# Two attention layers, one core: another place for the copied tiles and another order of the small products

## The reference

```python
# layer 0
theta, phi = W_theta x + b_theta, W_phi x + b_phi            # 64 channels
f = softmax(theta^T phi / sqrt(64))                          # 1024 x 1024 per image
x = x + W_fuse (x f^T) + b_fuse
# layer 1
h = group_norm(x, 32 groups) * gn_w + gn_b
q, k, v = q_w h + q_b, k_w h + k_b, v_w h + v_b              # 128 channels
a = softmax(q^T k / sqrt(128))
x = x + p_w (v a^T) + p_b
```

## Time and profile before

| | |
|---|---|
| median of 3 runs | 1895.29 us (1894.0 to 1898.93) |
| profiled execution | 1903.5 us, span 1901.7 us |
| busy | PE 92%, PEld 63%, DVE 75%, ACT 76%, POOL 67% |
| SP's DMA queue | 286.08 MB, 74.4% of 16 engines |
| granted TensorE clock | 0.990 of full speed |

### The profile page before, as it was taken

How to read it: one execution, slowest core, us unless ns; L and a number is a source line. 1 busy time by engine, 2 the same in 40 slices (tenths; PEclk the granted TensorE clock), 3 DMA queues, 4 the chain that set the end, 5 groups by cost and what they waited for, 6 DMA issues and landing times.

```text
span 1901.7 us, 34446 instructions
## 1 busy us (share of the span) xinstructions
PE 1759.0 (92%) x8966; PEld 1191.6 (63%) x8966; DVE 1432.4 (75%) x1650; ACT 1441.4 (76%) x2152; POOL 1273.3 (67%) x1321
## 2 busy tenths in 40 slices
PE   4799999999999999999999999999999999999986
PEld 2466666666666666666666666666666666666654
DVE  4577778778777787777787777877777878777854
ACT  3577877777877777877877877877887877877854
POOL 2566776666776666776666776666776666776652
PEclk9899999999999999999999999999999999999998
DMA  3578777877878778778777778778777777778764
GB/s 77 101 144 151 158 151 165 160 150 157 163 145 172 157 151 160 158 150 169 151 156 158 156 155 170 146 160 159 149 162 164 153 156 157 148 157 168 140 126 95
DMA packets 860085, 286.33 MB, mean 151 GB/s; under 512 B 822304, under 2 KB 823200, under 8 KB 860064
## 3 DMA queue, kind: packets, MB, share of 16 engines
q1 hardware_dynamic: 860064, 286.08, 74.4%
HBM read 50.86 MB, written 17.04 MB: 36 GB/s over the span
## 4 chain that ended last, share of the span: by engine, by line
issue 24%; DVE 17%; DMA 16%; ACT 14%; PE 11%; POOL 9%; SPq 9%; DVEq 1%; ACTq 0%; POOLq 0%
DMA et<-pair 11%; SPq L340 7%; DVE neg_max L704 6%; PE o_ps L416 5%; DMA rden_dram<-rden 4%; ACT s_ps L610 3%; ACT pair L635 3%; DVE pair L721 3%; DVE phi L795 2%; PE s_ps L416 2%; PE s_ps L454 2%; DVE x L758 2%; ACT et L620 2%; DVE x_max L781 2%; PE m_ps L416 1%
## 5 line engine op out<-in xcount | busy, mean ns | idle before, releaser
L416 PE MATMUL o_ps<-et,v_hi 128*128 128x512 f16 x2048 | 699.0, 383 | 50.3 <-DVE x L758 31.2
L704 DVE TENSOR_REDUCE neg_max<-s_ps 128x1 f32<-128x1024 f32 x512 | 624.4, 1220 | 66.0 <-PE s_ps L416 56.0
L416 PEld LDWEIGHTS o_ps<-et,v_hi 128*128 128x128 f16 x2048 | 203.0, 99 | 303.4 <-issue 119.8
L416 PE MATMUL o_ps<-et,v_lo 128*128 128x512 f16 x1024 | 390.6, 381 | 0.0
L721 DVE SCALAR_TENSOR_TENSOR pair<-s_ps,pair 128x1024 f16<-128x1024 f32 x256 | 312.1, 1219 | 75.6 <-ACT pair L635 74.4
L416 PE MATMUL s_ps<-phi,theta 128*128 128x512 f32 x1024 | 331.1, 446 | 6.0 <-ACT e_copied L610 3.7
L610 ACT ACTIVATE s_ps<-s_ps,neg_max 128x1024 f32<-128x1024 f32 x256 | 277.3, 1083 | 58.5 <-DVE neg_max L704 57.8
L846 POOL TENSOR_TENSOR pair<-e_copied,pair 128x1024 f16<-128x1024 f32 x128 | 274.6, 2145 | 23.3 <-ACT pair L633 23.3
L715 DVE SCALAR_TENSOR_TENSOR et<-s_ps,et 128x1024 f16<-128x1024 f32 x128 | 156.7, 1224 | 170.5 <-ACT et L620 170.5
L935 POOL TENSOR_TENSOR x<-x,xr 128x512 f32<-128x512 f32 x64 | 81.5, 1274 | 288.0 <-DVE x L758 288.0
L635 ACT ACTIVATE pair<-s_ps 128x1024 f16<-128x1024 f32 x256 | 262.2, 1024 | 8.1
(11 more groups left out here) (113 smaller groups left out, 3076.9 us busy)
## 6 DMA issues: line engine op xcount, KB each, us to landing
rden_row<-rden_dram SPq DMA_DIRECT2D x128, 256.0 KB, 3.9
xs<-in_x SPq DMA_DIRECT2D x32, 512.0 KB, 4.0
phi<-phi SPq DMA_DIRECT2D x64, 256.0 KB, 3.2
out_y<-y_sb SPq DMA_DIRECT2D x64, 256.0 KB, 2.5
et<-pair SPq DMA_TRANSPOSE x384, 4.6
rden_dram<-rden SPq DMA_DIRECT2D x128, 2.0 KB, 1.5
w_f<-in_w_fuse_t SPq DMA_DIRECT2D x1, 64.0 KB, 3.1
ident_sb<-in_ident SPq DMA_DIRECT2D x1, 64.0 KB, 2.3
```

Of the source, the lines that this page charges most:

```text
L416: mm = pe.matmul(out, lhs_t, rhs, start=start and n == 0, stop=stop and n == len(terms) - 1)
L704: nc.vector.tensor_reduce(neg_max[:, t % 4:t % 4 + 1], s_ps[:, part(t), :], AX.X, ALU.max, negate=True).then_inc(s_max, 1)
```

## The change

PAIRS becomes 4. Copied tiles use place 0 and place 3 in turn (a new function `place`), and every wait for a transpose and every transpose goes by the place. In UNITS w0 and q1 change slots (7 and 8), mx moves from slot 14 to slot 11 and v0 from 15 to 14; STAGE follows. On POOL the halves of h_lo are made in slots 2 and 3 instead of 3 and 4; in slot 2 this stands ahead of the copied tile's rest. The scores of slot 12 wait for one split more, since q1 comes a slot later.

```diff
-PAIRS = 3
+PAIRS = 4
-UNITS = {0: "gn1", 1: "gn2", 2: "v1", 4: "k0", 5: "k1", 6: "q0", 7: "q1", 8: "w0", 9: "w1", 10: "tp0", 12: "tp1",
-         14: "mx", 15: "v0"}
-STAGE = {"v1": 0, "k0": 1, "k1": 0, "q0": 1, "q1": 0, "w0": 1, "w1": 0, "v0": 1}
+UNITS = {0: "gn1", 1: "gn2", 2: "v1", 4: "k0", 5: "k1", 6: "q0", 7: "w0", 8: "q1", 9: "w1", 10: "tp0", 11: "mx",
+         12: "tp1", 14: "v0"}
+STAGE = {"v1": 0, "k0": 1, "k1": 0, "q0": 1, "w0": 0, "q1": 1, "w1": 0, "v0": 1}
-H_LO_SLOTS = (3, 4)
+H_LO_SLOTS = (2, 3)
...
+    def place(s):
+
+        return PAIRS - 1 if s % GROUP == COPIED and s // GROUP % 2 else s % GROUP
+
     def same_pair(s):
 
-        return lambda g: int(tile_at(g) and g % GROUP == s % GROUP)
+        return lambda g: int(tile_at(g) and g % GROUP != TURNED and place(g) == place(s))
...
                     if s == PHASE + GROUP:
-                        pe.wait_ge(s_split, before(staged_at, it, 8))
+                        pe.wait_ge(s_split, before(staged_at, it, 9))
...
-                n, r = before(tile_at, it, t), t % GROUP
+                n, r = before(tile_at, it, t), place(t)
                 act.wait_ge(s_exp, n + 1)
 
                 act.wait_ge(s_pair_t[r], 16 * before(same_pair(t), it, t))
...
-                    pool.wait_ge(s_h32, before(h_at, it, s))
-                    pool.wait_ge(s_hhi, before(h_at, it, s))
+                    pool.wait_ge(s_h32, before(h_at, it, H_SLOT) + 1)
+                    pool.wait_ge(s_hhi, before(h_at, it, H_SLOT) + 1)
...
-                        rest(pair[:, COPIED, 1, :], e_copied[:, :], pair[:, COPIED, 0, :], s_copied)
+                        rest(pair[:, place(t), 1, :], e_copied[:, :], pair[:, place(t), 0, :], s_copied)
```

More of the change, by code:

```diff
@@ L340, in move @@
                 sp.dma_start_transpose(et[:, t // GROUP % 4, r, :, :],
-                                       pair[:, r, :, :].rearrange("q a n -> q (a n)")).then_inc(s_pair_t[r], 16)
+                                       pair[:, place(t), :, :].rearrange("q a n -> q (a n)")).then_inc(
+                                           s_pair_t[place(t)], 16)
             def reciprocals_out(it, s):
@@ L463, in values @@
                 if quarter == 0:
-                    for r in range(PAIRS):
-                        pe.wait_ge(s_pair_t[r], 16 * before(same_pair(r), it, first + GROUP))
+                    for t in range(first, first + TURNED):
+                        pe.wait_ge(s_pair_t[place(t)], 16 * before(same_pair(t), it, first + GROUP))
                     pe.wait_ge(s_tlo, before(turned_at, it, first + GROUP))
```

## The result

| | before | after |
|---|---|---|
| median of 4 runs each | 1895.32 us | 1910.43 us (1908.19 to 1911.94) |
| ratio after/before | | 1.0074, interval 1.0058 to 1.0091 |
| profiled execution | 1903.5, span 1901.7 | 1908.19, span 1906.4 |

The changed kernel is slower by 15 us, 0.7%. So I compare one steady stretch of each instead, from VectorE's maximum of tile 0 in image 3 to the same in image 30: 27 images. One row for before, then one for after; the columns are the stretch, its length, the busy time of PE, PEld, DVE, ACT and POOL, the granted clock, the DMA share and GB/s.

What follows compares the result with a forecast made beforehand. Bound: VectorE in slots 10 to 15, the SP queue's reciprocals and transposes from slot 2 to 6. Terms +1.13 − 0.61 + 0.35 − 0.04 − 0.05 = +0.78 per image, times 30 = +23 us: 1918, range 1882 to 1930.

Steps and rivals of the forecast that it cites:

- Slot 6: Slot 6's value products: the third transpose's landing practically bounds them, so removing ScalarE's wait gives only −0.04 us per image.
- the transposes are not the bound of slot 6: Rival in slot 6: TensorE regains waits before q0 and k0; +0.08 us per image, 1898 us, no change; chance 0.12.
- The handshake: Slots 11 and 12: mx waits for VectorE's phi, VectorE's bound for mx; tile 11's turned rest +1.13 us per image.
- long way over TensorE: From mx in slot 11 through value products, tp1 and ScalarE to tile 11's turned rest: 519.45 where 518.32 stood, +1.13.
- the gain before it: VectorE's 0.46 us idle before tile 9's rest goes, so phi ends at 513.01 instead of 513.47.
- Slot 15: VectorE's bound (0.21) and clamp with reciprocal (0.40) leave slot 15: −0.61 us per image.
- v0's move: v0 in slot 14 fills TensorE's 1.05 us of waiting, but TensorE waits again before tile 15's transposes: 0.
- The queue: SP queue: transposes and xs load come 0.40 later against the next image's reciprocals: +0.35 us per image, ends 0 and +0.50.
- The fixed-cost rival: SP queue: about 2 us fixed per DMA, queue term 0; +0.43 per image, 1908 us; chance 0.64 together with the forecast.
- w0, q1 and h's low half: w0 before q1 in slots 7 and 8: −0.05 us per image; h's low half first on POOL: 0.
- The handshake costs nothing: Rival in slot 11: VectorE has taken phi before TensorE reaches mx; −0.60 us per image, 1877 us; chance 0.13.
- The queue gets worse: Rival: the handshake costs 0.90 and the late transposes 0.50; +1.30 us per image, 1934 us; chance 0.07.

Runs made afterwards that it cites:

- e3_mx_only: The kernel before with only mx moved to slot 11 and v0 to slot 14: 1949.87 us, ratio to before 1.0260.
- e9_small_parts: The kernel before with only w0 and q1 exchanged and h's low half in slots 2 and 3: 1900.42 us, ratio to before 1.0007.
- e7_xs_late: The changed kernel with the next image's xs load issued in slot 4 of the SP queue instead of slot 1: 1897.06 us, ratio to before 0.9974.
- e4_phi_first: The changed kernel with VectorE taking tp0's theta and phi before tile 9's rest in slot 11: 1897.49 us, ratio to before 0.9980.

## Why the prediction was right, and where its sizes were off

The direction and the mechanism held; 1918 was 8 too slow. Step by step, per image:

- **Slot 6: the transposes are the bound, though 131 us of ScalarE's waiting goes.** Held. Landing to first value product was 0.23 in the mean before and is 0.09 in 26 of 27 images after. The step was sized −0.04 and measured −0.14 (−0.12 in the mean over all 27). I had taken 0.2 as the price of waiting for a landing. In fact it was the end of a second chain that was just behind the landing. The ScalarE of before in that image:

```profile
548.07 1.06 ACT L633 ACTIVATE pair<-e_copied 128x1024 f16<-128x1024 f32 x1 [1.41 <-DMA et<-pair]
549.03 0.67 ACT L583 ACTIVATE stage<-m_ps,vec 128x512 f32<-128x512 f32 x1
```

The second transpose lands just before 548.07, the stage copy ends at 549.70, q0's product starts at 549.75, and behind its three matmuls the value product at 550.56. After, q0's product starts at 552.20 and TensorE stands 0.76 before the value product. This is the slack that the removed wait left unused; the rival "the transposes are not the bound of slot 6" falls by it.

- **The handshake.** Forecast +1.13 from slot 10's normalisation to the turned rest, measured +0.97. Its long way over TensorE was forecast at 1.59 (1.13 + 0.46) and measured at 1.56, and VectorE's wait for the bound at 0.55 and measured 0.58 in every image. The step that was mis-sized is the gain before it: phi comes 0.60 earlier by the normalisation, not 0.46. VectorE's idle time before tile 9's rest was 0.50 in the mean over images (0.41 to 1.02); I had sized it from one image. The remaining 0.10 I did not trace. A slip in the working is small: it takes 0.98 from tp1's start to ScalarE's theta, where its rows give 1.02 (514.84 to 515.86).

- **Slot 15.** Forecast −0.61, measured −0.67. v0's move gave nothing else, as forecast: TensorE waits 1.23 before tile 15's transposes in every image (0.33 in the mean before), and they start no earlier after it. That is a reading of the timelines; no run moves v0 alone.

- **The queue.** Forecast +0.35, measured +0.31 at the third landing. That the two are so close is partly luck: the price was taken from two images of one kernel, and e3_mx_only, whose lead shrinks by 0.47 instead of 0.44, has 0.65. The fixed-cost rival fell, although its 1908 is nearer to the measured 1910 than my 1918: other terms moved the number there, and its own term, 0, is not what the queue shows. The time of the 2 KB out went from 2.29 to 2.58 with the load nearer, and to 1.72 where the load is elsewhere. The Trainium skill ("DMA: Bandwidth & Descriptors", section on queues, rings and completion order) says that a DMA engine's semaphore write lands only after its earlier writes; these numbers agree with it, and so do the landings of the 2 KB 0.35, 0.26 and 0.19 behind that of the load. The Trainium skill gives the rival's 2 us (same page, section on the anatomy of one DMA) for DMAs that GpSimd issues. Those here are issued by SP, and in slot 10, where everything ahead of them had landed, the 2 KB took 1.64 before and 1.63 after.

- **w0, q1 and h's low half.** Forecast −0.05 together, and e9_small_parts measures none. Tile 0's rest ends 2.0 later (10.85 to 12.82), where I had 1.8. h's low half costs only when the reciprocals come back early, as e7_xs_late shows.

The terms make +0.11 up to slot 10, +0.97 and −0.67: +0.41, where the forecast had +0.26, +1.13 and −0.61. Two thirds of the missing 0.37 lie in gains of the fourth place that I undersized (0.10 in slot 6, 0.14 before phi). "The handshake costs nothing" fell by the row of mx. "The queue gets worse" was right in kind for e3, where its term was 0.65.

One thing in the comparison of profiles is the clock's. Behind the maximum of image 31 the span goes on for 120.6 us before and 113.7 after, although little is changed there. e9_small_parts, whose steady part is that of before, takes 115.4. The rows of these ends (stretch, length, busy times, granted clock, DMA share, GB/s), for before and e9:

```profile
1781.10:1901.70 120.60, 97.41 (x452) 61.93 (x451) 63.35 (x69) 65.87 (x100) 62.87 (x67) 0.92 0.58 118
```

```profile
1781.20:1896.60 115.40, 91.54 (x451) 57.99 (x451) 63.22 (x68) 65.56 (x99) 62.79 (x67) 0.98 0.61 124
```

TensorE works on the same matmuls in both (one is missing from the second), but it is busy 97.41 us at a mean clock of 0.92 and 91.54 at 0.98. That is 5.9 more, and the end is 5.2 longer. The changed kernel's end had a mean clock of 0.96. So a difference of two spans was not fit to size the change.

## What to carry to other kernels

A wait total says how long an engine stood, not what anyone gains: look at the consumer and ask which second chain ends just behind the one removed. Before a small product is moved into a slot, look at what its single bank waits for in that slot, since everything queued behind it on the in-order engine pays. And test the parts of a change alone: this one held a part that gives 1.0% and one that costs 2.6%.

## What the runs showed that I had not expected

The 2 KB of reciprocals of slots 2 and 6 take 1.7 to 1.9 us from issue to landing where the load is not ahead of them, 2.3 to 3.2 with the 512 KB load 2.2 to 1.2 us ahead, and 3.8 to 4.2 with the load and a store ahead. The load is not alone in this: in slot 14 of e4_phi_first, with a copy of phi 1.1 ahead, they take 2.30 instead of 1.62 after. Moving the load took this time out of slot 2 but put it on something else each time. And the same handshake costs +1.57 per image in one surrounding and +0.93 in another (57.30 against 56.37, the full change against the fourth place alone). Half of the difference lies in the queue: the third transpose lands 0.65 later in the one and 0.32 in the other. The lead that the image's end leaves shrinks by about the same in both (0.47 and 0.51), so it is not the cause, which stays open.
